# Normalising, transposing and first projecting the tokens by pairs of blocks, with every other block normalised by ScalarE

## What is computed

```python
xn = _layernorm(x, axis=-1)                     # (x - mean) / sqrt(var + 1e-5), per token
qkv = xn @ Wqkv                                 # 256 -> q1, k1, q2, k2 (128 each), v (256)
A1 = _causal_sdpa(q1, k1, v)                    # 16 heads, head size 8, values 16 wide
A2 = _causal_sdpa(q2, k2, v)
diff = A1 - lam * A2                            # then rms-normed per head
attn = diff @ Wproj
ff_gate = _qdot(xn, w_gating[0])                # fp8 inputs
ff1 = _qdot(xn, w_gating[1])
ffn = _qdot(gelu(ff_gate) * ff1, w_linear)
out = x + attn + ffn
```

## Time and profile before

| | us |
|---|---|
| median of 3 runs (198.6 to 199.15) | 198.92 |
| the profiled execution | 199.27 |
| its span in the trace | 197.5 |
| PE busy | 182.2 (92%) |
| ACT busy | 163.6 (83%) |
| DVE busy | 92.4 (47%) |
| POOL busy | 59.4 (30%) |

### The profile page before, as it was taken

How to read it: one execution, slowest core, us unless ns; L and a number is a source line. 1 busy time by engine, 2 the same in 40 slices (tenths; PEclk the granted TensorE clock), 3 DMA queues, 4 the chain that set the end, 5 groups by cost and what they waited for, 6 DMA issues and landing times.

```text
span 197.5 us, 3554 instructions
## 1 busy us (share of the span) xinstructions
PE 182.2 (92%) x1446; PEld 78.3 (40%) x1450; DVE 92.4 (47%) x218; ACT 163.6 (83%) x136; POOL 59.4 (30%) x71
## 2 busy tenths in 40 slices
PE   6899989899999999999989999999998999899940
PEld 6855334454332323242333424344342423233830
DVE  0975798431223240540472025216703697895840
ACT  2156865899999999999999999999999899998010
POOL 8526600042216142314442043235216124320000
PEclk9999999999999999999999999999999999999997
DMA  5967377780000000000277781000000000000051
GB/s 174 404 242 245 73 179 205 207 190 10 0 0 3 0 0 3 0 0 3 60 203 188 181 191 39 0 3 0 0 3 0 0 3 0 0 3 0 0 178 44
DMA packets 8149, 14.99 MB, mean 76 GB/s; under 512 B 1984, under 2 KB 5312, under 8 KB 8128
## 3 DMA queue, kind: packets, MB, share of 16 engines
q1 hardware_dynamic: 7440, 14.05, 25.5%
q10 hardware_dynamic: 688, 0.66, 1.0%
HBM read 5.26 MB, written 1.05 MB: 32 GB/s over the span
## 4 chain that ended last, share of the span: by engine, by line
PE 74%; ACT 15%; DVE 4%; POOL 1%; issue 1%; POOLq 0%; DVEq 0%
PE ps L910 29%; PE ps L898 17%; ACT probs L442 13%; PE ps L752 8%; PE ps L758 4%; PE ps L941 4%; PE ps L747 3%; PE ps L851 3%; PE ps L813 3%; DVE area L529 2%; DVE o_t L594 1%; ACT probs L430 1%; PE ps L742 1%; PE ps L947 1%; ACT L430 1%
## 5 line engine op out<-in xcount | busy, mean ns | idle before, releaser
L442 ACT ACTIVATE probs<-ps,shift 128x1536 f32<-128x1536 f32 x96 | 140.1, 1554 | 2.4 <-PE ps L898 1.6
L910 PE MATMUL ps<-probs,v_all 128*32 128x512 f32 (+3 forms) x768 | 78.1, 496 | 1.5 <-DVE o_t L594 1.5
L366 POOL TENSOR_SCALAR_AFFINE_SELECT probs<-probs 128x1024 f32<-128x1024 f32 (+1 forms) x40 | 36.7, 917 | 109.7 <-ACT probs L442 109.6
L898 PE MATMUL ps<-q_st,k_st 32*128 32x512 f32 (+3 forms) x384 | 49.8, 420 | 1.2 <-issue 0.8
L898 PEld LDWEIGHTS ps<-q_st,k_st 32*128 32x128 f32 x384 | 22.4, 182 | 58.6 <-ACT probs L442 30.4
L594 DVE STREAM_TRANSPOSE o_t<-ps 128x512 f32<-128x512 f32 x16 | 11.5, 717 | 49.5 <-PE ps L910 49.5
L910 PEld LDWEIGHTS ps<-probs,v_all 128*32 128x32 f32 x768 | 16.4, 108 | 19.6 <-issue 13.9
L752 PE MATMUL ps<-xn_t,w_q 128*128 128x512 f32 (+1 forms) x38 | 17.3, 557 | 0.8 <-ACT xn_t L393 0.8
L813 PE MATMUL ps<-area 128*128 128x512 fp8e4 x64 | 14.5, 379 | 1.0 <-DVE area L529 1.0
L430 ACT ACTIVATE probs<-ps 128x512 bf16<-128x512 f32 x16 | 9.3, 597 | 4.5 <-PE ps L813 2.7
L529 DVE TENSOR_TENSOR area<-ps,probs 128x512 fp8e4<-128x512 f32 x16 | 10.5, 687 | 1.8 <-ACT probs L430 1.7
(11 more groups left out here) (78 smaller groups left out, 117.2 us busy)
## 6 DMA issues: line engine op xcount, KB each, us to landing
q_st<-parts SPq DMA_DIRECT2D x32, 128.0 KB, 2.8
k_st<-parts SPq DMA_DIRECT2D x32, 128.0 KB, 2.8
probs<-L_ffn_w_gating SPq DMA_DIRECT2D x4, 512.0 KB, 7.8
probs<-L_ffn_w_linear SPq DMA_DIRECT2D x1, 1024.0 KB, 13.1
w_q<-L_attn_Wqkv SPq DMA_DIRECT2D x2, 384.0 KB, 5.8
out<-probs SPq DMA_DIRECT2D x3, 256.0 KB, 3.0
x_sb<-L_attn_x SPq DMA_DIRECT2D x2, 256.0 KB, 4.2
x_sb<-L_attn_x ACTq DMA_DIRECT2D x2, 256.0 KB, 4.5
```

The source lines that it names most:

```text
L366: pool.affine_select(out=blocks, in_=blocks, pattern=pattern, compare_op=ALU.is_ge, fill=0.0, base=0, channel_multiplier=-1).then_inc(mask ...
L442: act.activation(probs[:, at:at + PER_UNIT, :].rearrange("p s u -> p (s u)"), ps[:, 3 * (n % 2):3 * (n % 2) + 3, :].rearrange("p b n -> p ...
L898: ins = pe.matmul(ps[:, bank, at:at + wide * P], k_st[rows, g % STACKS, kb * P:(kb + 1) * P], q_st[rows, g % STACKS, queries], start=True, ...
L910: ins = pe.matmul(ps[32 * j:32 * j + 32, 6, q0 % HALF:q0 % HALF + wide * P], v_all[:, g % HG, kb, 32 * j:32 * j + 32], probs[:, slot + j, ...
```

## The change

The opening goes by pairs of blocks (256 tokens) in place of halves. In each pair DVE normalises the even block, as before by subtract and multiply, and ACT the odd one, by an activation `Identity` with scale `1/sigma` and bias `-mean/sigma`, for which DVE makes the bias in `rstd[:, 3]`. Both chunks of a pair are transposed into one bank and copied by one ACT instruction of 2x256 columns. Units 0 and 1 are projected in two parts of 256 columns each, one part per pair. The values of blocks 0 and 1 stand between and behind the transposes of the third and the fourth pair; `norms_of(0)` stands behind `unit(2)`. DVE's order behind the normalisation, POOL's and SP's are as they were.

The diff, cut to its core:

```diff
@@ ScalarE
-            def turned(h):
-                act.wait_ge(xt_ready, h + 1)
-                for k in range(KC):
-                    act.activation(xn_t[:, k, h * HALF:(h + 1) * HALF], ps[:, 2 * h + k, :], ACT.Copy
-                                   ).then_inc(xt_out, 1)
+            def odd_block(i):
+                b = 2 * i + 1
+                act.wait_ge(moved_ready, i + 1)
+                act.activation(xn[:, b, :], x_sb[:, b, :], ACT.Identity, bias=rstd[:, 3, b:b + 1],
+                               scale=rstd[:, 2, b:b + 1]).then_inc(odd_ready, 1)
+            def turned(i):
+                act.wait_ge(xt_ready, i + 1)
+                act.activation(xn_t[:, :, i * C:(i + 1) * C], ps[:, i, :].rearrange("p (k n) -> p k n", k=KC), ACT.Copy
+                               ).then_inc(xt_out, 1)
@@ VectorE
+            def even_block(i):
+                b = 2 * i
+                dve.wait_ge(root_ready, i + 1)
+                own.step(dve.reciprocal(rstd[:, 2, b:b + 2], rstd[:, 1, b:b + 2]))
+                dve.scalar_tensor_tensor(rstd[:, 3, b + 1:b + 2], mean_var[:, b + 1, 0:1], -1.0, rstd[:, 2, b + 1:b + 2],
+                                         ALU.mult, ALU.mult).then_inc(moved_ready, 1)
+                dve.tensor_scalar(xn[:, b, :], x_sb[:, b, :], mean_var[:, b, 0:1], rstd[:, 2, b:b + 1],
+                                  ALU.subtract, ALU.mult).then_inc(even_ready, 1)
             stats_of(0)
...
+            spread_of(0)
+            for i in range(1, TB // 2):
+                stats_of(i)
+                even_block(i - 1)
+                spread_of(i)
+            even_block(TB // 2 - 1)
...
-                dve.wait_ge(xt_out, (h + 1) * KC)
+                dve.wait_ge(xt_out, 2 * (h + 1))
@@ TensorE
             transposes(0)
             pe.wait_ge(wq_in, 32)
-            unit(0)
-            unit(1)
-            transposes(1)
+            for i in range(2):
+                if i == 1:
+                    transposes(1)
+                pe.wait_ge(xt_out, i + 1)
+                for u in range(2):
+                    for k in range(KC):
+                        ins = queries_keys(u, QK_BANK[u], k, i * C, C)
+                    if i == 1:
+                        ins.then_inc(qk_ready, 1)
+            transposes(2)
+            project_values(0, 6)
+            transposes(3)
+            project_values(1, 6)
+            unit(2)
             pe.wait_ge(picks_set, BR)
             norms_of(0)
-            project_values(0, 6)
-            project_values(1, 6)
-            unit(2)
             pe.wait_ge(low_ready, 1)
             norms_of(1)
             unit(3)
-            pe.wait_ge(xt_out, 2 * KC)
             norms_of(2)
```

More of the change, by code:

```diff
@@ L191, in diff_attention_ffn_kernel @@
         mean_var = sb("mean_var", [P, TB, 2], F32)
-        rstd = sb("rstd", [P, 3, TB], F32)
+        rstd = sb("rstd", [P, 4, TB], F32)
         lam_in = sb("lam_in", [P, 4, DK], F32)
@@ L218, in diff_attention_ffn_kernel @@
         dve_general = [dve_general0, sem("dve_general1")]
-        var_ready, root_ready, xn_ready, xt_ready, xt_out, x8_ready = (sem(n) for n in (
-            "var_ready", "root_ready", "xn_ready", "xt_ready", "xt_out", "x8_ready"))
+        var_ready, root_ready, moved_ready, even_ready, odd_ready, xt_ready, xt_out, x8_ready = (sem(n) for n in (
+            "var_ready", "root_ready", "moved_ready", "even_ready", "odd_ready", "xt_ready", "xt_out", "x8_ready"))
         qk_ready, hi_ready, low_ready, v_ready, v_out = (sem(n) for n in (
@@ L385, in _, with root @@
                 act.dma_start(x_sb[:, b:b + 2, :], x_rows[:, b:b + 2, :]).then_inc(x_in[b // 2], 16)
-            def root(h):
-                act.wait_ge(var_ready, h + 1)
-                act.activation(rstd[:, 1, 4 * h:4 * h + 4], rstd[:, 0, 4 * h:4 * h + 4], ACT.Sqrt).then_inc(root_ready, 1)
-            def turned(h):
-                act.wait_ge(xt_ready, h + 1)
-                for k in range(KC):
-                    act.activation(xn_t[:, k, h * HALF:(h + 1) * HALF], ps[:, 2 * h + k, :], ACT.Copy
-                                   ).then_inc(xt_out, 1)
+            def root(i):
+                act.wait_ge(var_ready, i + 1)
+                act.activation(rstd[:, 1, 2 * i:2 * i + 2], rstd[:, 0, 2 * i:2 * i + 2], ACT.Sqrt).then_inc(root_ready, 1)
+            def odd_block(i):
[7 more added lines that the diff above has]
+                               ).then_inc(xt_out, 1)
             def upper(u):
@@ L408, in _ @@
             root(0)
+            odd_block(0)
+            root(1)
             turned(0)
-            root(1)
+            odd_block(1)
+            root(2)
+            turned(1)
+            odd_block(2)
+            root(3)
             upper(0)
+            odd_block(3)
+            upper(1)
+            turned(2)
+            turned(3)
             square_of(0)
-            upper(1)
-            turned(1)
             square_of(1)
@@ L470, in _, with stats_of, spread_of @@
             own = Own(dve, dve_own)
-            def stats_of(h):
-                for b in range(4 * h, 4 * h + 4):
+            def stats_of(i):
+                for b in range(2 * i, 2 * i + 2):
                     dve.wait_ge(x_in[b // 2], 16)
                     own.mark(dve.bn_stats(stats[:, b, :], x_sb[:, b, :]))
+            def spread_of(i):
                 own.wait()
-                for b in range(4 * h, 4 * h + 4):
+                for b in range(2 * i, 2 * i + 2):
                     own.mark(dve.bn_aggr(mean_var[:, b, :], stats[:, b, :]))
                 own.wait()
-                dve.tensor_scalar(rstd[:, 0, 4 * h:4 * h + 4], mean_var[:, 4 * h:4 * h + 4, 1], EPS, None, ALU.add
+                dve.tensor_scalar(rstd[:, 0, 2 * i:2 * i + 2], mean_var[:, 2 * i:2 * i + 2, 1], EPS, None, ALU.add
                                   ).then_inc(var_ready, 1)
-            stats_of(0)
[L484 to L491, removed]
+            def even_block(i):
[6 more added lines that the diff above has]
+                                  ALU.subtract, ALU.mult).then_inc(even_ready, 1)
+            stats_of(0)
+            spread_of(0)
[4 more added lines that the diff above has]
+            even_block(TB // 2 - 1)
             def rest(u, bank):
@@ L736, in _, with transposes @@
             pe.wait_ge(ident_set, 1)
-            def transposes(h):
-                for b in range(4 * h, 4 * h + 4):
-                    pe.wait_ge(xn_ready, b + 1)
+            def transposes(i):
+                for e in range(2):
+                    pe.wait_ge((even_ready, odd_ready)[e], i + 1)
                     for k in range(KC):
-                        ins = pe.transpose(ps[:, 2 * h + k, (b % 4) * P:(b % 4 + 1) * P],
-                                           xn[:, b, k * P:(k + 1) * P], ident[:, :])
+                        ins = pe.transpose(ps[:, i, k * C + e * P:k * C + (e + 1) * P],
+                                           xn[:, 2 * i + e, k * P:(k + 1) * P], ident[:, :])
                 ins.then_inc(xt_ready, 1)
@@ L770, in unit @@
                 h = QK_UNITS[u][1]
+                pe.wait_ge(xt_out, 2 * (h + 1))
                 for k in range(KC):
-                    pe.wait_ge(xt_out, h * KC + k + 1)
                     ins = queries_keys(u, QK_BANK[u], k, 0, HALF)
```

## The result

The changed kernel takes **205.02 us** in the median of six executions (201.77 to 206.82), against 199.0 (198.6 to 199.22): slower, by 3.0% in the medians. The ratio given with the result, 1.0215 (95% interval 1.0149 to 1.0281), counts only the three executions within 1.5% of the fastest, 201.77, 203.36 and 204.65. The forecast was 202.3, range 200.2 to 202.9: the right side, but too small. The spread had grown from 0.6 us to 5. The single executions took 203.36, 204.65, 206.82, 205.39, 205.48 and 201.77; the profile is of the first.

What follows compares the result with a forecast made beforehand. PE, not normalisation, was taken to bound the opening, with no slack behind it. Feed-forward step 4 moves from 24.27 to 27.74, +3.47, taken as +3.4: 198.92 + 3.4 = 202.3 us, range 200.2 to 202.9.

Steps and rivals of the forecast that it cites:

- The bound, and that the opening passes on one for one: PE, not normalisation, bounds the opening; exponentials have no slack, so its loss or gain reaches the end one for one.
- Second gap: In the projections: PE idles 0.92 us more, since the projection after the second transposes needs exactly their copy.
- Cost of `Identity`: ACT's normalisation of an odd block, without a row in the profile: taken as 0.39 us, bounds 0.33 to 0.63.
- First transposes at 8.24, "unchanged": PE's opening: transposes start when the identity products let them, at 8.24 us as before.
- DVE first: Rival: DVE's second-half fp8 cast precedes POOL's `w_linear` cast, which waits at no cost: +1.64, 200.6 us, chance 0.34.
- The forecast hangs on 20.03 against 20.00: DVE's second-half fp8 cast comes up at 20.03 us, POOL's `w_linear` cast at 20.00; the margin is smaller than the rounding.
- POOL first: Main case: DVE's second-half fp8 cast waits for POOL's whole 1.89 us `w_linear` cast: +3.47, taken as +3.4, chance 0.52.
- step 0: First feed-forward step on PE: forecast to start at 23.9 us with POOL first, 22.1 with DVE first.
- the analogy of 1.0 us of idle time: PE idles 2.4 us ahead of feed-forward; clock stayed 1.00 at 28 to 30 us, PE busy 0.99 of 2.00: nothing added.
- From 40 us on, all rows as before, later by the loss: Expected sign in the profile: behind the opening nothing changes except a shift by the opening's loss.

Runs made afterwards that it cites:

- a_less4_late8: `a_less4` with DVE's fp8 cast of the second half moved between its third and fourth maximum: 200.03 us against 199.05, ratio 1.0045.
- a_less4_gap: `a_less4` with the second pair's transposes moved between the first parts of units 0 and 1: 199.6 us against 199.39.
- a_less4: The changed kernel with four DVE instructions fewer in the skipped general path of the second branch: executions 205.24, 205.04, 200.27 and 204.18 us.
- b_more4: The kernel before with four more DVE instructions in the skipped path of the second branch: 200.69 us against 199.39, ratio 1.0077.
- b_more124: The kernel before with 124 more DVE instructions in the skipped path of the second branch: 200.4 us against 199.05, ratio 1.0062.

## Why the prediction was wrong

- **The bound, and that the opening passes on one for one: right** as far as 120 us. Exponentials start 1.02 late, and at 99.24 the offset is 1.03.
- **Second gap: right.** From the start of those transposes to the next projection it was 1.28 (10.86 to 12.14) against 0.44 + 0.92 = 1.36 in the sum, and covering it gave back about 0.8 (1.0 above before in `a_less4_late8`, 0.2 in `a_less4_gap`; they differ in the place of DVE's cast as well).
- **Cost of `Identity`: in its bounds.** The four took 0.59 to 0.60, not the 0.39 taken. One stood ahead of an `upper`, but DVE idled 3.19 for the first norms behind that, so it hid.
- **First transposes at 8.24, "unchanged": the first step that failed.** With 18 products they start from 7.26 to 8.55 in the traces. With 7.68 the sum for DVE first, +1.64, becomes +1.08; 1.02 was measured. So that sum was right, and its starting point was one draw of a quantity that moves by 1.3 us.
- **"The forecast hangs on 20.03 against 20.00": right, and then misused.** Both sides move (DVE's cast 19.26 to 20.29, POOL's 19.27 to 19.76 in unforced profiles), so neither case is the result; both are, execution by execution. Two groups of times some 2 us apart by its own sums (+1.64 and +3.4), and a spread to match, should have been forecast.
- **Price of POOL first, +3.4: too small, and enough to make it wrong.** The three slower executions of `a_less4`, one with a trace, stand 4.8 to 5.9 above before, so its median, 204.61, is past the range without any wait at the jump. The term had POOL's cast and not the memset behind it (step 0 0.66 later than forecast), and it added nothing for the clock, by the analogy of 1.0 us of idle time; 2.78 were followed by 3.4 us at 1.2 GHz, worth 1.6. Together 3.4 + 0.7 + 1.6 = 5.7, and 5.8 was measured.
- **"From 40 us on, all rows as before, later by the loss": the other step that made it wrong.** The sum counted only what is executed. Four more instructions on DVE moved the target of a jump, and 2.5 us of waiting came at 120 us. That is worth 1.3 to 1.6 by `b_more4`, and was 3.1 where the clock fell behind it, as in the profiled execution. There DVE was first, so it is this step alone that puts 203.36 outside the range.

Together: 199.0 + 1.0 + 1.4 = 201.4 is near the fastest execution, 201.77; with the clock's fall 199.0 + 4.1 = 203.1 is near the profiled one, 203.36. With POOL first and the jump, 204.6 + 1.4 = 206.0 is among the upper four (204.65 to 206.82). That those had POOL first is inferred from `a_less4`; they have no trace.

Their mean granted clocks fit this. A fall of 3.4 us to one half takes about 0.0085 off the mean over 200 us (an estimate, 3.4/2/200). The fastest and 204.65 have 0.993, so probably no fall; 203.36 has 0.980 with one in its trace; 205.39 and 205.48 have 0.985 and 0.979; 206.82 has 0.972, room for two. But the executions of the kernel before vary from 0.987 to 0.995, as much as one fall, so this supports the account and does not prove it.

## What to carry to other kernels

Count the instructions that a change adds ahead of a jump, also where none of them is on the critical path: here the place of the code behind a jump cost 1.3 to 1.6 us, more than the 1.0 that the change itself cost with DVE first. When two casts of DVE and POOL come up within the spread of their starts, forecast two groups of times, and move one of them away rather than hope for the order. Work that is ready early gains nothing while filler ahead of it sets the start: change both together, with the filler alone as the control.

## What the runs showed of the hardware

- Behind a taken jump DVE stood 1.2 to 1.7 us when the target was instruction 450 or 451 of its program, and 3.7 to 3.8 when it was 454 or 574. In the long waits an instruction packet came 1.75 to 2.0 us ahead of the first copy behind the jump; in the short ones none came.
- A DVE fp8 cast waited for POOL's cast and for a memset that followed it at once (2.95 for 0.68 of work); it went on when that memset ended. When the memset was not there it waited for the cast alone (2.35).
- The granted clock was at 0.50 for 3.4 us after PE had idled 1.50 (changed kernel), 2.43, 2.78 and 3.59 (the three traces with POOL first), and it stayed at 1.00 after 1.0. After 1.49 in `b_more4` and 1.42 in `b_more124` it stayed at 1.00 as well, so idle time near 1.5 us was followed by a fall in one trace of three.
- The pace of the first identity products rises from some 4 to 7 records per half us, at an instant between 5 and 7.5 us that differs between executions, while the granted clock reads 1.00 throughout.
